# Regrouping queries, keys, values and outputs from SBUF to SBUF instead of through DRAM

## The reference

```python
Q = (x @ Wq.T).reshape(b, s, 16, 16)          # K, V likewise
scores = jnp.einsum('bshd,bstd->bsht', Q, K) / math.sqrt(16)
attn = jax.nn.softmax(scores, axis=-1)
out = jnp.einsum('bsht,bstd->bshd', attn, V).reshape(b, s, 256)
x = layernorm(x + out @ Wfc.T)
topk_idx, topk_w = route(x)                   # 4 of 32 experts per token
mixed = sum over the 4 of topk_w * down_e(silu(gate_e(x)) * up_e(x))
x = layernorm(x + mixed + shared_expert(x))
```

## Time and profile before

| | us |
|---|---|
| median of 3 runs (lowest to highest) | 580.22 (578.54 to 580.25) |
| profiled execution | 585.22 |
| its span (first to last instruction) | 583.4 |
| TensorE busy in the span | 532.9 |
| VectorE / ScalarE / GpSimd busy | 353.0 / 296.2 / 285.1 |
| DMA queue of SyncE (q1), share of 16 engines | 52.6% |
| DMA queue of ScalarE (q10) | 7.5% |

### The profile page before, as it was taken

One profiled execution on the slowest core, in us unless ns is written; L12 is line 12 of the kernel. 1 busy time (PEld: TensorE's weight loads), 2 busy tenths in 40 slices (PEclk: granted clock), 3 DMA queues, 4 the chain that ended last, 5 costly groups with the idle time before them and its releaser, 6 DMA issues.

```text
span 583.4 us, 16223 instructions
## 1 busy us (share of the span) xinstructions
PE 532.9 (91%) x4604; PEld 402.9 (69%) x4605; DVE 353.0 (61%) x1207; ACT 296.2 (51%) x641; POOL 285.1 (49%) x293
## 2 busy tenths in 40 slices
PE   5989999997979999789888999999999999988994
PEld 2445667565647566556445999999988888877883
DVE  2032647897876899677943444444446666555865
ACT  1324463765646574423403566666655555545454
POOL 5000000664676767567770466666666655555400
PEclk9999999998989999899997999999999999999999
DMA  7998998997697999799623354555577777778398
GB/s 252 250 245 201 235 258 200 275 258 219 206 273 241 275 272 406 258 405 348 232 102 85 112 152 144 161 183 171 160 224 227 226 238 222 230 220 295 138 386 292
DMA packets 132219, 135.31 MB, mean 232 GB/s; under 512 B 77128, under 2 KB 115535, under 8 KB 131536
## 3 DMA queue, kind: packets, MB, share of 16 engines
q1 hardware_dynamic: 105984, 87.53, 52.6%
q0 software_dynamic: 12672, 34.10, 15.4%
q10 hardware_dynamic: 13520, 13.13, 7.5%
HBM read 74.79 MB, written 60.96 MB: 233 GB/s over the span
## 4 chain that ended last, share of the span: by engine, by line
PE 49%; DMA 18%; DVE 14%; SPq 6%; issue 6%; ACT 3%; DVEq 2%; ACTq 1%; POOL 1%; POOLq 0%
PE bank L1003 44%; DMA o_slots<-wgu_sb 5%; DMA prod<-expert_rows 5%; PE bank L1359 3%; DMA wd_sb<-o_slots 3%; DMA wgu_sb<-pick_rows 2%; SPq L368 1%; DVEq L299 1%; DMA pick_rows<-prod,ids 1%; ACT sx L972 1%; SPq L359 1%; DVE hsT L1527 1%; DMA wqkv_sb<-in_wqkv 1%; DVE hsT L1524 1%; SPq L522 1%
## 5 line engine op out<-in xcount | busy, mean ns | idle before, releaser
L616 POOL DMA_INDIRECT pick_rows<-prod,ids x134 | 139.2, 1039 | 101.8 <-ACT prod L929 75.8
L582 POOL DMA_INDIRECT expert_rows<-stage,pos x128 | 127.2, 994 | 58.9 <-issue 36.4
L1003 PE MATMUL bank<-prod 128*128 128x128 f32 x1088 | 134.8, 278 | 0.6 <-DVE prod L1845 0.6
L1003 PEld LDWEIGHTS bank<-prod 128*128 128x128 f32 x1088 | 129.0, 194 | 1.0 <-issue 0.9
L1003 PE MATMUL bank<-wd_sb,wqkv_sb 128*128 128x512 f32 x192 | 91.9, 615 | 6.3 <-DMA wqkv_sb<-in_wqkv 6.3
L1845 DVE COPY prod<-wgu_sb 128x512 f32 x136 | 54.0, 438 | 67.7 <-issue 59.3
L929 ACT ACTIVATE prod<-bank,kept 128x256 f32<-128x256 f32 x136 | 57.3, 470 | 31.3 <-PE bank L1003 27.7
L1003 PEld LDWEIGHTS bank<-wgu_sb 128*32 128x32 f32 x2048 | 58.8, 136 | 20.2 <-issue 17.0
L1003 PE MATMUL bank<-wgu_sb 128*32 128x64 f32 x2048 | 66.2, 296 | 4.6 <-DMA wgu_sb<-k_slots 3.7
L1003 PE MATMUL bank<-wd_sb,prod 128*128 x272 | 70.1, 380 | 0.4 <-DVE prod L1863 0.4
L1003 PEld LDWEIGHTS bank<-wd_sb,wqkv_sb 128*128 128x128 f32 x192 | 35.2, 195 | 42.5 <-issue 36.1
(11 more groups left out here) (170 smaller groups left out, 650.9 us busy)
## 6 DMA issues: line engine op xcount, KB each, us to landing
prod<-expert_rows SPq DMA_DIRECT2D x136, 132.0 KB
wsgu_sb<-pick_rows ACTq DMA_DIRECT2D x32, 256.0 KB, 3.8
wgu_sb<-pick_rows SPq DMA_DIRECT2D x12, 512.0 KB, 10.7
wgu_sb<-in_wgu SPq DMA_DIRECT2D x2, 2560.0 KB, 13.1
expert_rows<-pad_rows SPq DMA_DIRECT2D x4, 1056.0 KB, 19.1
wd_sb<-in_xT SPq DMA_DIRECT2D x8, 512.0 KB, 5.0
q_slots<-wd_sb SPq DMA_DIRECT2D x16, 256.0 KB
k_slots<-wd_sb SPq DMA_DIRECT2D x16, 256.0 KB, 4.2
```

The source lines that it names most:

```text
L582: pool.indirect_dma_start(xs, bass.IndirectOffsetOnAxis(ap=pos[e % 2][:, i, k:k + 1], axis=0), stage[:, i, k, :], None, bounds_check=XROWS ...
L616: pool.indirect_dma_start(z, bass.IndirectOffsetOnAxis(ap=index[:, j:j + 1], axis=0), rows[:, j, :], None, bounds_check=TOPK * NTOK - 1, o ...
L1003: return pe.matmul(dst, lhsT, rhs, start=(k == 0), stop=(k == n - 1))
```

## The change

The four DRAM tensors and their writes and reads are gone. In their place each slot is moved by one DMA from SBUF to SBUF: 8 for queries, 8 for keys and 8 for values per chunk, issued by SyncE, and 8 for the outputs, issued by ScalarE right behind its second `copy_o` of the chunk. `QT`, `KT` and `VT` get a second place for odd chunks, in parts of `sx` that only chunks 5 to 7 need (and `xT_sb[0]` for the values of chunk 7), so that `evacuate` waits for the regrouping two chunks back, and `normalise` of chunks 5 to 7 waits for the regrouping that still reads there. The order of features in the weights is arranged on the host so that the direct transfers put them where the matmuls want them. SyncE's list is shorter, with the same loads in it; TensorE's, VectorE's and GpSimd's lists are as before.

```diff
-            def write_slots(dram, tensor, n, done, landed):
...
-            def read_q(n):
...
-            def read_o(n):
...
+            def regroup_q(n):
+                sp.wait_ge(S["evac"], 6 * n + 2)
+                if n:
+                    sp.wait_ge(S["s_ready"], 2 * n)
+                for t in range(SLOT):
+                    sp.dma_start(Q2[t * HD:(t + 1) * HD, (t // 4) * 1024:(t // 4 + 1) * 1024],
+                                 qT_of(n)[:, :, slot(t)]).then_inc(S["q_in"], 16)
+            def regroup_k(n):
+                sp.wait_ge(S["evac"], 6 * n + 4)
...
+            def regroup_v(n):
+                sp.wait_ge(S["evac"], 6 * n + 6)
+                if n:
+                    sp.wait_ge(S["o_ready"], 2 * n)
...
+            regroup_q(0)
+            regroup_k(0)
             load_xT(2)
-            write_v(0)
             load_x(0)
+            regroup_v(0)
             load_x(1)
             load_xT(3)
+            regroup_q(1)
+            regroup_k(1)
+            regroup_v(1)
             load_xT(4)
+            regroup_q(2)
+            regroup_k(2)
             load_xT(5)
+            regroup_v(2)
             load_x(2)
+            regroup_q(3)
+            regroup_k(3)
             load_x(3)
+            regroup_v(3)
+            regroup_q(4)
+            regroup_k(4)
             load_xT(6)
             load_x(4)
+            regroup_q(5)
+            regroup_k(5)
+            regroup_v(4)
             load_xT(7)
             load_x(5)
...
             def evacuate(a, j):
                 act.wait_ge(S["proj_ready"], 6 * a + j + 1)
-                if a and j % 2 == 0:
-                    act.wait_ge(S[("q_wr", "k_wr", "v_wr")[j // 2]], (64 if j == 4 else 32) * a)
+                if a >= 2 and j % 2 == 0:
+                    act.wait_ge(S[("q_in", "k_in", "v_in")[j // 2]], IN * (a - 1))
...
+            def regroup_o(n):
+                act.wait_ge(S["o_copied"], 2 * (n + 1))
+                if n >= 2:
+                    act.wait_ge(S["y_ready"], 2 * (n - 1))
+                for t in range(SLOT):
+                    act.dma_start(OT[n % 2][:, :, t * GRP:(t + 1) * GRP], O_sb[t * NH:(t + 1) * NH, :])\
+                        .then_inc(S["o_in"], 16)
...
             def normalise(b):
+                if b >= CH - 3:
+                    act.wait_ge(S[("v_in", "k_in", "q_in")[b - (CH - 3)]], IN * (CH - 2 if b == CH - 3 else CH))
...
             copy_o(0, 1)
+            regroup_o(0)
             evacuate(3, 1)
             exponents(1, 0)
...
             copy_o(4, 1)
+            regroup_o(4)
             stage_rows(2, range(0, 1))
             copy_ranks(2)
...
             def score(p, hf):
-                pe.wait_ge(S["q_rd"], 32 * (p + 1))
-                pe.wait_ge(S["k_rd"], 128 * (p + 1))
+                pe.wait_ge(S["q_in"], IN * (p + 1))
+                pe.wait_ge(S["k_in"], IN * (p + 1))
...
             def out_project(b, pair):
-                pe.wait_ge(S["o_rd"], 32 * (b + 1))
+                pe.wait_ge(S["o_in"], IN * (b + 1))
```

More of the change, by code:

```diff
@@ L88, in build @@
     z = nc.dram_tensor("pick_rows", [TOPK * NTOK, DM], F32).ap()
[L89 to L92, removed]
     with ExitStack() as ctx:
@@ L173, in x1_of, with qT_of, kT_of, vT_of @@
             return over(sx, b * TPC * DM, TPC, DM)
+        def qT_of(n):
+            return over(sx, (CH - 1) * TPC * DM, KC, CT) if n % 2 else QT
+        def kT_of(n):
+            return over(sx, (CH - 2) * TPC * DM, KC, CT) if n % 2 else KT
+        def vT_of(n):
+            if n == CH - 1:
+                return xT_sb[0]
+            return over(sx, (CH - 3) * TPC * DM, KC, CT) if n % 2 else VT
         stage = sb("stage", [P, TPC, TOPK, ROW])
@@ L278, in build @@
         NSMALL = 5 * 16
+        IN = SLOT * 16
         NCONST = 13
@@ L343, in read_q, with slot @@
-            def read_q(n):
-                sp.wait_ge(S["q_wr"], 32 * (n + 1))
+            def slot(n):
+                return slice(n * GRP, (n + 1) * GRP)
+            def regroup_q(n):
+                sp.wait_ge(S["evac"], 6 * n + 2)
                 if n:
                     sp.wait_ge(S["s_ready"], 2 * n)
[L347 to L350, removed]
@@ L362, in read_v @@
-            def read_v(n):
-                sp.wait_ge(S["v_wr"], 64 * (n + 1))
+                for t in range(SLOT):
+                    sp.dma_start(K2[t * HD:(t + 1) * HD, (t % KB) * 1024:(t % KB + 1) * 1024],
+                                 kT_of(n)[:, :, slot(t)]).then_inc(S["k_in"], 16)
+            def regroup_v(n):
+                sp.wait_ge(S["evac"], 6 * n + 6)
                 if n:
                     sp.wait_ge(S["o_ready"], 2 * n)
[L366 to L369, removed]
@@ L371, in write_o @@
-            def write_o(n):
-                sp.wait_ge(S["o_copied"], 2 * (n + 1))
-                sp.dma_start(o_slots[n].rearrange("t (h d) g -> (t h) (d g)", d=HD), O_sb).then_inc(S["o_wr"], 16)
-            def read_o(n):
[L376 to L381, removed]
+                for t in range(SLOT):
+                    sp.dma_start(V2[t * NH:(t + 1) * NH, (t // 2) * 1024:(t // 2 + 1) * 1024],
+                                 vT_of(n)[:, :, slot((t % 2) * 4 + t // 2)]).then_inc(S["v_in"], 16)
@@ L465, in _ @@
[L465 to L482 removed]
+            regroup_q(6)
@@ L483, in _ @@
+            regroup_v(5)
+            regroup_k(6)
+            load_x(6)
+            regroup_v(6)
+            regroup_q(7)
+            regroup_k(7)
+            load_x(7)
+            regroup_v(7)
             sp.wait_ge(S["s_ready"], 2 * CH)
```

117 lines of the change are left out of this document (25 added, 92 removed).

## The result

The changed kernel takes 605.66 us (median of 4 runs, 604.82 to 610.66), the kernel before 580.24 in the runs beside it (4 runs, 578.54 to 581.45). The ratio is 1.0458, with a 95% interval of 1.0395 to 1.0522: 25.4 us slower, where 4 us faster was forecast. The profiled execution took 606.44, its span 604.7, and the rows of the kernel after are of this one.

A forecast was written before the change was run, and what follows sets the result against it. TensorE was taken to bound the attention phase, with a ceiling of 18.7 us; 2.6 + 0.76 - 0.3 + 1.2 = 4.3 us were to be won, 580.2 - 4.3 = 576 us. Range 571 to 579; 8 in 10, 565 to 587.

The forecast's parts named there:

- I take 0.5, so A = 4.0 us per chunk: A is ScalarE's time for issuing 8 output DMAs per chunk, at 0.5 us each; bounds 3.4 to 8.5 us.
- the prediction's own formula: Whole attention phase: gain = 4.3 - 4 (A - 4.0) us, A being ScalarE's issue time per chunk.
- The sum moves by four times A: Last four chunks, each at ScalarE's pace: gain 6.7 us at A = 3.4, zero at A = 5.1.
- all but 0.3 us in chunk 1: ScalarE in chunks 0 to 2: idle time covers the issues; only `out_project(1, 0)` loses 0.3 us, between 0 and 1.
- 1.6 us won: Chunk 7: ScalarE's idle 2.1 us covers half the issues; `out_project(7, 0)` at 241.9 instead of 243.45, 1.6 left on TensorE.
- Chunk 6, "Left: 0": `copy_ranks(4)` on ScalarE, done at 211.5, just meets `place(4)` on VectorE at 211.54; no lead of TensorE remains.
- a direct transfer as slow as both legs: Rival: landing 5 us behind the last issue, `K2` late at every `score`, 580 to 584; no chance of its own.
- at 0.47 us each ... I cost this at nothing: SyncE's 24 issues per chunk: 16 fit before the next `score`, 9.8 against 10.9 us at the tightest, so no loss.
- the first `score`: Chunk 0: queries and keys land some 10 us before TensorE needs them, so its wait on `K2` goes, winning 2.6 us.
- `project(6, 4)` and `turn(4, 0)` as places where ScalarE is late: Signs of a right forecast: new TensorE waits on ScalarE's copies at these two and, third, at `router(6)`.
- the DMA share in 60 to 90: Sign of a right forecast: the DMA engines' share from 60 to 90 us falls well under 0.97.
- issues above 0.63 us, a wait of `score` on `K2`: Signs of a wrong forecast: ScalarE's issues dearer than 0.63 us each, or TensorE's `score` waiting for keys.

The follow-up runs named there:

- e4: Kernel before with only the outputs direct, 8 issues per chunk by ScalarE, early expert weights held behind o of chunk 6: 595.31 us, ratio 1.0197.
- e8: As e4, with every output transfer cut in two, 16 DMAs of 32 KB per chunk: 636.98 us, ratio 1.0906.
- e1: Changed kernel with the two early loads of expert weights held behind the landing of o of chunk 6: 595.62 us, ratio 1.0218.
- e3: Changed kernel with the outputs through DRAM again, written and read by SyncE; queries, keys and values direct, early loads not held: 606.94 us, ratio 1.0391.
- e10: e1 with the outputs issued by halves, 4 by ScalarE and 4 by SyncE per chunk: 586.14 us, ratio 1.0078.
- e7: As e4, but SyncE issues 4 of the 8 output transfers of a chunk and ScalarE the other 4: 578.60 us, ratio 0.9911.
- e2: Changed kernel with the two early weight loads at their old place, cut into 12 and 10 DMAs in pieces of 2 KB: 596.58 us, ratio 1.0215.
- e11: Probe: e7 plus eight series of 8 DMAs on ScalarE's queue at its end; total not compared, SBUF-to-SBUF issues 0.64 to 0.71 us.

## Why the prediction was wrong, by its own steps

*"I take 0.5, so A = 4.0 us per chunk".* This is the mis-sized term. It measured 0.64 and 6.2: with the time from one issue to the next eight take 5.3, and single issues of up to 1.86 us make the rest. The row from which 0.5 came is of 132 KB, not 64, with an end in DRAM; for straight 64 KB the probe has 0.45 with such an end and 0.67 without. The bounds of 3.4 to 8.5 held 6.2; the value taken from between them did not. The upper bound was read wrongly: the four issues of 4.27 us were not 1.07 each, but one of 2.89 and three of some 0.42. By the prediction's own formula 6.2 gives 4.3 - 4 x 2.2 = 4.5 us lost, some 585: the sign turns with this term alone, as the text said it would from 0.63.

*"The sum moves by four times A".* Too flat. e4 and e8 stand 41 us apart for 4.4 us of A: more than eight chunks' full blocks (8 x 4.4 = 35). The forecast let chunks 0 to 2 hide their blocks, all but 0.3 us in chunk 1, and counted no clock on the new waits. In the changed kernel chunk 1 loses 3.1: from `out_project(0, 0)` to `out_project(1, 0)` it takes 27.8 us where the kernel before takes 24.7. In chunk 7 the forecast looked at `router(6)` and put 1.6 us won; but `copy_ranks(5)` stands behind the same block of issues, TensorE waits for it at `shared_down(0, 1)` (4.62 in e1, 3.92 in the changed kernel), and from `out_project(6, 0)` to `out_project(7, 0)` e1 takes 29.8 us where the kernel before takes 25.2. Together the two places are about the 8 us that e1, without the collision, costs beyond the formula (12.6, where it gives 4.5 at A = 6.2). In e8 TensorE waits 4.87 at 68.04 and 5.02 at 97.83 for ScalarE too (rows of the same kind as the one shown), and the matmuls behind such waits run at the lower clock (3.41 us, at 0.56 granted, for four that take 1.88 in the earlier trace rows).

*Chunk 6, "Left: 0".* This is the step that failed outright, for 14 of the 25 us. The prediction followed ScalarE's work behind the issues and asked which engine waits. It did not ask what the transfers had been queued behind, and ahead of. As long as SyncE issued both, its queue kept `o` of chunk 6 ahead of 5.5 MB of weights in pieces of 20 and 24 KB; in e3, with that order and the loads not held, the wait is 1.40 us. Issued by ScalarE, `o` meets them, and the wait is 14.29. The prediction had no rival of that kind; its "a direct transfer as slow as both legs" allowed 5 us for a landing that took 19.

*SyncE "at 0.47 us each ... I cost this at nothing; at 0.6 us per issue it would be 1 us late, at this one place".* It is 0.62 each, 0.65 with the time to the next, and the wait is 2.19, at `score(4, 0)` and not at `score(5, 0)`. It stays small in the changed kernel while ScalarE is later still: in e10, where ScalarE is relieved, it is 8.9 us in five places.

*Right:* the first `score`, 2.6 us won (it starts at 32.97 without a wait, at 35.64 before); `project(6, 4)` and `turn(4, 0)` as places where ScalarE is late (5.57 and 4.17), though not the third, `router(6)`, where the changed kernel has no wait; the DMA share in 60 to 90 (0.58); the rule by which the forecast would fall, "issues above 0.63 us, a wait of `score` on `K2`": both came.

Of the two rules of the Trainium skill that the prediction weighed, both in "DMA: Bandwidth & Descriptors", the section "Issuing engines are not separate DMA queues" calls the sequencer time that further issuing engines save usually small beside the transfer. The runs disagree for 64 KB: moving half of the issues to another engine is worth 2.9% (e4 to e7). The Trainium skill's section "Rules for kernel authors" on the same page asks to join small transfers. The runs agree: cutting these in two cost 7% (e4 to e8).

What stays open: how the DMA engines share their time between the two queues (e2 changed the size of the pieces and, with it, the pace at which loads start), why an issue with an end in DRAM takes 0.42 for one transfer and 0.60 for another, and whether another placing in SyncE's list would bring direct queries and keys to a gain.

## What to carry to other kernels

A transfer that moves to another engine's queue costs that engine the full issue time of every DMA in it, and delays whatever work stands behind it without a gap. So count DMAs and not bytes, price them from a row of the same kind (both ends, size, shape), look at every instruction behind the block and not only at the next, and split a block between two queues where neither has a gap for the whole. And a queue is also an order: before a small transfer is taken out of it, look at what large load stands next in it, for outside it only a semaphore holds the two apart, as in e1.

## What the runs showed of the hardware

- An issue from SBUF to SBUF takes 0.64 to 0.71 us on ScalarE's queue, from 256 B to 256 KB alike, and 0.45 for straight 64 KB with one end in DRAM, with nothing else under way (e11, means of eight).
- 0.21 MB in pieces of 256 B on one queue took 18 us beside 5.53 MB on another, mostly in pieces of 20 and 24 KB, and cost TensorE 14.29 us. With that load in pieces of 2 KB, started one after the other, the wait was 1.13 (e2); with `o` ahead of the load in the same queue it was 1.40 (e3).
